# Cross-attention on one core: where in SBUF the scores' weights lie, and a layer norm in place

## What is computed

```
Q = x @ Wq ; K = ctx @ Wk ; V = ctx @ Wv            (per head)
attn = softmax(mask(Q K^T / 16)) ; c = attn V
out = concat_heads(c) @ Wo + x
y = (out - mean(out)) * rsqrt(var(out) + 1e-5) * gamma + beta
```

## Time and profile before

| | |
|---|---|
| median of three executions | 318.01 us |
| the profiled execution's own time | 317.95 us |
| its span in the profile | 316.1 us |
| TensorE busy (weight loads) | 309.5 us (303.4 us) |
| VectorE, ScalarE, GpSimd busy | 253.1, 222.0, 181.3 us |

### The profile page before, as it was taken

The page is one execution under the profiler, slowest core; times in us unless marked ns, Lnnn a source line. Parts: engine busy times, 40 slices in busy tenths (PEclk is TensorE's granted clock), DMA queues, the critical chain, the costliest instruction groups (busy, mean ns, idle before and its releaser), DMA issues.

```text
span 316.1 us, 8051 instructions
## 1 busy us (share of the span) xinstructions
PE 309.5 (98%) x2584; PEld 303.4 (96%) x2584; DVE 253.1 (80%) x721; ACT 222.0 (70%) x601; POOL 181.3 (57%) x183
## 2 busy tenths in 40 slices
PE   8999999999999999999999999999999999999993
PEld 7998889999999999999999999999999999999992
DVE  0467778777999789987998889987998889975686
ACT  2446677768867787678777797678767887777640
POOL 1123476457864587558855586558755686457212
PEclk9999999999999999999999999999999999999998
DMA  7996443564354454384446535364355435440101
GB/s 254 358 400 242 137 150 117 158 218 134 98 163 160 159 175 140 141 239 142 133 126 208 172 133 163 129 214 156 113 187 185 170 100 184 143 155 4 35 0 66
DMA packets 46911, 50.27 MB, mean 159 GB/s; under 512 B 3504, under 2 KB 37040, under 8 KB 46896
## 3 DMA queue, kind: packets, MB, share of 16 engines
q1 hardware_dynamic: 46608, 49.56, 47.0%
q10 hardware_dynamic: 288, 0.52, 0.7%
HBM read 32.24 MB, written 17.83 MB: 158 GB/s over the span
## 4 chain that ended last, share of the span: by engine, by line
PE 95%; DMA 2%; DVE 1%; SPq 1%; POOLq 0%; issue 0%; POOL 0%
PE score_bank L321 25%; PE out_bank L321 19%; PE gL_bank L321 14%; PE tL_bank L321 13%; PE tU_bank L321 9%; PE gU_bank L321 7%; DMA wq_raw<-in_wqT 2%; PE spare_bank L321 1%; PE tL_bank L355 1%; PE spare_bank L355 1%; PE tL_bank L337 1%; PE tU_bank L337 1%; PE out_bank L361 1%; PE tU_bank L361 1%; PE out_bank L337 0%; PE spare_bank L337 0%
## 5 line engine op out<-in xcount | busy, mean ns | idle before, releaser
L1017 POOL TENSOR_TENSOR probs<-probs,inv_sum 128x512 f32<-128x512 f32 x64 | 66.7, 1043 | 84.4 <-DVE inv_sum L804 83.8
L615 ACT ACTIVATE probs<-neg_scores,neg_max 128x256 f32<-128x256 f32 x128 | 64.1, 502 | 36.1 <-DVE neg_max L793 36.0
L1040 POOL TENSOR_TENSOR pT_lo<-pT_raw,pT_hi 128x512 fp32r<-128x512 f32 x60 | 76.6, 1297 | 8.6 <-ACT pT_hi L572 8.6
L793 DVE CUSTOM_DVE_ANT_0 neg_scores<-score_bank,mask_bias 128x256 f32<-128x256 f32 x128 | 49.1, 420 | 6.3 <-PE score_bank L321 3.9
L814 DVE STREAM_TRANSPOSE squares<-probs 128x512 f32<-128x512 f32 x60 | 42.3, 706 | 1.0 <-DMA scratch<-squares 0.8
L572 ACT ACTIVATE tL_hi<-tL_bank 128x512 fp32r<-128x512 f32 x31 | 18.6, 599 | 29.6 <-PE tL_bank L321 29.6
L321 PE MATMUL score_bank<-ctxT_hi,gU 128*128 128x256 f32 x128 | 36.1, 282 | 0.0
L321 PE MATMUL score_bank<-ctxT_hi,gL_lo 128*128 128x256 f32 x128 | 35.9, 281 | 0.0
L321 PE MATMUL score_bank<-ctxT_lo,gU 128*128 128x256 f32 x128 | 35.9, 281 | 0.0
L321 PE MATMUL score_bank<-ctxT_lo,gL_hi 128*128 128x256 f32 x128 | 35.9, 280 | 0.0
L321 PE MATMUL score_bank<-ctxT_hi,gL_hi 128*128 128x256 f32 x128 | 35.6, 278 | 0.0
(11 more groups left out here) (167 smaller groups left out, 981.0 us busy)
## 6 DMA issues: line engine op xcount, KB each, us to landing
scratch<-squares SPq DMA_DIRECT2D x30, 512.0 KB, 2.8
pT_raw<-scratch SPq DMA_DIRECT2D x120, 128.0 KB, 3.1
xT_raw<-in_xT SPq DMA_DIRECT2D x8, 256.0 KB, 4.5
ctxT_raw<-in_ctxT SPq DMA_DIRECT2D x8, 256.0 KB, 4.7
wo_raw<-in_wo SPq DMA_DIRECT2D x4, 512.0 KB, 14.3
x_res<-in_x SPq DMA_DIRECT2D x8, 256.0 KB, 3.2
out<-y_out SPq DMA_DIRECT2D x7, 256.0 KB, 2.6
wq_raw<-in_wqT SPq DMA_DIRECT2D x3, 512.0 KB, 7.6
```

The source lines that it names most:

```text
L615: nc.scalar.activation(probs[j % 2][:, n, :], neg_scores[:, n, :], ACT.Exp, bias=neg_max[:, n:n + 1], scale=-1.0, accum_out=row_sum[:, n:n ...
L793: nc.vector.tensor_tensor_reduce(out=neg_scores[:, n, :], in0=score_bank[hh][:, q, :], in1=mask_bias[:], scale=-SCALE, scalar=3.0e38, op0= ...
L1017: nc.gpsimd.tensor_tensor(probs[j % 2][:, rows, :], probs[j % 2][:, rows, :], inv, ALU.mult) \
L1040: nc.gpsimd.tensor_tensor(pT_lo[j % 2][:, k].rearrange("p hh (q i r) -> p (hh q) i r", q=QT, i=ROWS), pT_raw[j % 2][:, k].rearrange("p i n ...
```

## The change

- The g tiles lose their padding and move ahead of tL_hi, among the other weights, at a remainder of 0. With the 64 bytes of eps_col and power_col left between the weights and all that is streamed, every distance becomes 64 instead of -64.
- Steps 0 to 4 use another buffer for g, `g_early`, which lies right ahead of the streamed tiles at the same remainder as these: distance 0 in their scores.
- The layer norm works in place in `y`: y_scaled and y_out are gone, the store reads `y`, and the wait for the previous store moves from the normalisation to the addition of the residual.
- The last batch's sum, statistics and result are in `y_last`, which now lies in the probabilities' first buffer.

```
-APART = 16
+EARLY = 5
+        gL_hi = sb("gL_hi", [P, 2, S], F32R)
+        gL_lo = sb("gL_lo", [P, 2, S], F32R)
+        gU = sb("gU", [P, 2, S], F32R)
         tL_hi = sb("tL_hi", [P, 2, S], F32R)
...
         power_col = sb("power_col", [P, QT])
-        gL_hi = sb("gL_hi", [P, 2, S + APART], F32R)[:, :, 0:S]
-        gL_lo = sb("gL_lo", [P, 2, S + APART], F32R)[:, :, 0:S]
-        gU = sb("gU", [P, 2, S + APART], F32R)[:, :, 0:S]
+        g_early = sb("g_early", [P, 3, 2, S], F32R)
         xT_hi = sb("xT_hi", [P, IT, S], F32R)
...
         y = sb("y", [P, QT, DI])
-        y_scaled = sb("y_scaled", [P, QT, DI])
-        y_out = sb("y_out", [P, QT, DI])
-        y_last = neg_scores[:, 0:QT, :]
...
+        y_last = probs[0][:, 0:QT, :]
+        def g_tiles(t):
+            if isinstance(t, int) and t < EARLY:
+                return tuple(g_early[:, n] for n in range(3))
+            return gL_hi[:], gL_lo[:], gU[:]
...
-                sp.dma_start(batch_of(out, b), y_out[:]).then_inc(out_stored, 16)
+                sp.dma_start(batch_of(out, b), y[:]).then_inc(out_stored, 16)
...
                 dve.wait_ge(out_product, PAIRS * b + PAIRS)
+                dve.wait_ge(out_stored, 16 * b + 16)
                 nc.vector.tensor_tensor(y[:], out_bank[:], x_res[:], ALU.add).then_inc(out_bank_read, 1)
...
-            def centre_tile(q):
+            def centre_tile(rows, q):
                 nc.vector.scalar_tensor_tensor(
-                    y_scaled[:, q, :], y[:, q, :], mean_var[:, q, 0:1], gamma_sb[:],
+                    rows[:, q, :], rows[:, q, :], mean_var[:, q, 0:1], gamma_sb[:],
...
-            def normalise_tile(b, q, into):
+            def normalise_tile(b, q, rows):
                 nc.vector.scalar_tensor_tensor(
-                    into[:, q, :], y_scaled[:, q, :], rstd[:, q:q + 1], beta_sb[:],
+                    rows[:, q, :], rows[:, q, :], rstd[:, q:q + 1], beta_sb[:],
...
                 dve.wait_ge(rstd_done, b + 1)
-                dve.wait_ge(out_stored, 16 * b + 16)
```

More of the change, by code:

```diff
@@ L384, in scores @@
             def scores(t, j, b, heads=(0, 1)):
+                L_hi, L_lo, U = g_tiles(t)
                 if j == 0:
@@ L395, in scores @@
                         rows = slice(q * P, (q + 1) * P)
-                        hi, lo, up = gL_hi[:, hh, rows], gL_lo[:, hh, rows], gU[:, hh, rows]
+                        hi, lo, up = L_hi[:, hh, rows], L_lo[:, hh, rows], U[:, hh, rows]
                         split_products(score_bank[hh][:, q, :],
@@ L599, in gU_hi_part @@
                 act.wait_ge(g_product, 2 * t + 1)
-                hi_part(gU[0:UP, 0, :], gU_bank[0:UP, 0, :]).then_inc(g_hi_done, 1)
-                hi_part(gU[UP:P, 1, :], gU_bank[UP:P, 0, :]).then_inc(g_hi_done, 1)
+                U = g_tiles(t)[2]
+                hi_part(U[0:UP, 0, :], gU_bank[0:UP, 0, :]).then_inc(g_hi_done, 1)
+                hi_part(U[UP:P, 1, :], gU_bank[UP:P, 0, :]).then_inc(g_hi_done, 1)
             def gL_hi_part(t):
                 act.wait_ge(g_product, 2 * t + 2)
-                hi_part(gL_hi[:], gL_bank[:]).then_inc(g_hi_done, 1)
+                hi_part(g_tiles(t)[0], gL_bank[:]).then_inc(g_hi_done, 1)
             def exponentials(t, j, heads=(0, 1)):
@@ L775, in gU_lo_part @@
                 own, other = (slice(0, UP), slice(UP, P))[::1 if hh == 0 else -1]
-                lo_part(gU[other, hh, :], gU_bank[own, 0, :], gU[own, hh, :]).then_inc(g_split, 1)
+                U = g_tiles(t)[2]
+                lo_part(U[other, hh, :], gU_bank[own, 0, :], U[own, hh, :]).then_inc(g_split, 1)
             def gL_lo_part(t):
                 dve.wait_ge(g_hi_done, 3 * t + 3)
-                lo_part(gL_lo[:], gL_bank[:], gL_hi[:]).then_inc(g_split, 1)
+                L_hi, L_lo, _ = g_tiles(t)
+                lo_part(L_lo, gL_bank[:], L_hi).then_inc(g_split, 1)
             def maxima(t, b, heads=(0, 1)):
@@ L883, in centre @@
                         dve.wait_ge(mean_done, QT * b + QT)
-                    centre_tile(q)
+                    centre_tile(y, q)
             def normalise(b):
                 dve.wait_ge(rstd_done, b + 1)
-                dve.wait_ge(out_stored, 16 * b + 16)
                 for q in range(QT):
-                    normalise_tile(b, q, y_out)
+                    normalise_tile(b, q, y)
             def step(t, j, b, ends=None, folds=()):
@@ L982, in _ @@
                     dve.wait_ge(x_res_in, 16 * B)
-                nc.vector.tensor_tensor(y[:, q, :], output(STEPS - 1, q), x_res[:, q, :], ALU.add) \
+                nc.vector.tensor_tensor(y_last[:, q, :], output(STEPS - 1, q), x_res[:, q, :], ALU.add) \
                     .then_inc(out_bank_read, 1)
                 dve.wait_ge(out_bank_read, B + 1 + q)
-                nc.vector.bn_stats(stats[:, q, :], y[:, q, :]).then_inc(stats_done, 1)
+                nc.vector.bn_stats(stats[:, q, :], y_last[:, q, :]).then_inc(stats_done, 1)
                 dve.wait_ge(stats_done, QT * (B - 1) + 1 + q)
@@ L992, in _ @@
                 dve.wait_ge(mean_done, QT * (B - 1) + 1 + q)
-                centre_tile(q)
+                centre_tile(y_last, q)
             for q in range(QT):
```

## The result

The changed kernel takes 324.75 us (median of four, 324.51 to 324.93) against 318.0; the ratio is 1.021, 95% interval 1.0198 to 1.0222. It is 2.1% slower. The forecast was 315.4; the rival "slow for good" had stood at 324.5.

What follows compares the result with a forecast made beforehand. TensorE, busy 98% of the span, was taken to bound the kernel by its matmul pitch. Terms -2.9 + 0.3 = -2.6 us against the profiled 317.95 gave 315.35, stated as 315.4 for the median; range 314.6 to 321.5.

Steps and rivals of the forecast that it cites:

- slow for good: Rival: scores of steps 0 to 4 hand over the slow rhythm and nothing ends it; 324.5 us, chance 0.15.
- What bounds the kernel, and the two rhythms: TensorE's pitch sets the time; rhythms of 113.3 and 117.6 ns hold themselves; scores' excess costs 0.107 us a step.
- Distance 64 in steps 5 to 31: Scores join the fast rhythm, steps become 8.613 us: -2.9 us, bounds -2.9 and +5.7.
- Distance 0 in steps 0 to 4: 100 early score products at 120.0 ns each: +0.3 us, bounds -0.4 and +0.7.
- What these scores hand over: Step 4's scores at distance 0, followed by query products at 64, were taken to hand over the fast rhythm.
- The sign: Distances outside the scores turn from -64 to 64; fast products at -64 were taken as guide, no separate price.
- VectorE's lead: At step 9's gL_lo load, 0.20 us of lead less 0.17 saved by TensorE leaves 0.03: no wait, cost 0.
- fast throughout: The main case: the fast rhythm holds from the handover on; 314.6 to 316.0 us, chance 0.66.
- The layer norm and the end: Moved store wait never waits, at most some 0.05 us a batch; products behind the final transposes stay slow; 0 taken.
- The rule of two independent read ports: Skill's rule that weight loads take nothing from the running matmul: SBUF places without effect, time stays 318; prediction disagreed.

Runs made afterwards that it cites:

- e1: Changed kernel with g_early padded as before: old mixture of distances in scores of steps 0 to 4, -64 elsewhere; 314.84 to 317.40 us, one execution 323.14.
- e9: e1 plus one needless VectorE addition in step 5 between the low parts of gU and gL, making TensorE wait; 320.09 and 321.43 us.
- e8: e1 with 128 bytes of gap ahead of g_early: same mixture in steps 0 to 4, but distance 64 elsewhere; 324.52 us.
- e10: Changed kernel with 384 bytes of gap ahead of g_early: distance 0 in scores of steps 0 to 4, -64 elsewhere; 324.68 us.
- e5: Changed kernel with distance 0 in scores of steps 0 to 5 (EARLY = 6); five of six executions 323.20 to 323.92 us, one 316.16.
- e14: e1 repeated unchanged; 322.64, 315.02, 315.23, 315.20 and 315.49 us.
- e2: Kernel before with only the in-place layer norm and y_last in the probabilities; 318.08 us, ratio 1.0006.
- e3: Changed kernel with distance 64 in the scores of all steps, 0 to 4 included (EARLY = 0); 324.83 us.
- e7: e1 with the old mixture of distances also in the first step of every batch (g_early where j = 0); 315.86 to 316.23 us, ratio 0.993.
- e4: Changed kernel with distance 0 in the scores of every step (g_early always used); 319.22 us, ratio 1.0037.
- e11: e5 with the layer norm's centring moved behind the low parts of g on VectorE; 325.23 us.
- e6: Changed kernel with distance 0 in step 5's scores alone, distance 64 in all other steps; 323.55 and 323.61 us.
- e12: e1 with the layer norm's centring moved behind the low parts of g on VectorE; 322.66 us.

## Why the prediction was wrong, point by point

- *What bounds the kernel, and the two rhythms.* Right. TensorE's pitch is the time; 113.3 and 117.8 ns both hold themselves, and the 0.107 us a step is there to be had (e1).
- *Distance 64 in steps 5 to 31.* Forecast -2.9 with bounds -2.9 and +5.7; it came out beyond the upper one: +6.01 for the 26 steps between the starts of steps 5 and 31, where the bound gives 26 x 0.21 = +5.5. The slow pitch is 117.8 ns and not the 117.5 that I took from two-digit lengths, which makes 0.231 us a step.
- *Distance 0 in steps 0 to 4.* Forecast +0.3. The five pieces of the chain sum to 12.81 us against 12.58, +0.23. Right.
- *What these scores hand over.* This is the step that failed: "None shows 0 followed directly by 64. I take fast." I had taken distance 0 for a disturbance that ends any rhythm. It has two sequences of its own, and step 4 gets the one that hands over slow: its query products take 1.41 us for 12 and not 1.36, and the steps behind them 8.95 us and not 8.61. The place from which I read that an even run ends fast had a wait between, and e9 shows that such a wait often ends fast by itself. I gave the rival 0.15 though its ground, "nothing ends it any more", stood on rows and my own choice did not. That its 324.5 lies so near the 324.75 is in part luck: it has 0.3 us for slow query products in steps 0 to 3, which were fast, and its steps were priced 0.02 us too low.
- *The sign.* I treated 64 like -64. e8 and e10 show that both the mixture and distance 0 hand over differently to the two.
- *VectorE's lead.* 0.03 us forecast to be left; in e5 and e14 it is used up and TensorE waits 0.02. The sum left out a term: the load starts 0.05 us after gL_lo ends even when TensorE is waiting for it (the kernel before shows it too, in step 1), so 0.20 - 0.17 - 0.05 = -0.02 us. By this the change would have met the wait even with a fast handover, as e5 did, and "fast throughout" at 0.66 was too high on this ground too. In the changed kernel the point never comes up, since its slow steps leave VectorE ahead.
- *The layer norm and the end.* Right (e2; the end is slow as before). The +0.21 us behind the start of step 31 is mostly that step's output and context products, now slow too.
- *The rule of two independent read ports* (the Trainium skill, "TensorE: Matmul & The Clock Gate", section "Step-by-step: what each phase is for"). By it the time would not have moved. The same matmuls at other addresses take 315.2 (most executions of e1 and e14), 318.0 (before) or 324.8 us (after, e3) here.

What stays open is what the phase consists of: no row shows the reads themselves, so why an entry gives one sequence or the other can be tested but not foreseen from these traces. A rival to "distance" also stands untested. The places are worked out from the order of the buffers, and in every kernel here the streamed tiles begin at remainder 64 or 448, both odd multiples of 64. An even distance therefore always goes with weights that begin at an odd multiple of 64 bytes, and the sign with where the streamed tiles lie. No run moves weights and streamed tiles together, so whether the difference counts or the places themselves is not shown.

## What to carry to other kernels

A chain of equal matmuls with a weight load each held either of two pitches for hundreds of products here. Before disturbances are taken away, ask what sets the good rhythm and what sets it again after a wait: here the slower scores of the kernel before were also its repair. A short repair in each round (0.1 us of 34.5) was worth more than the last 0.1 us: e7's six executions have a mean of 316.0 us, the 11 of e1 and e14, without the repair, 316.8. One execution does not show how often a rhythm is lost. And where a lead is worked out from two engines' rows, take off the time from the end of the one's instruction to the start of the other's when it does wait.

## What the runs showed of the hardware that was not expected

- Where the weights being loaded and the streamed operand lie in SBUF changes a matmul's pitch: 113.3 or 117.8 ns at distances of 64 and -64, 120.0 at distance 0 (after, e1, e3, e4). Whether the difference of the two places counts or the places themselves was not tested.
- A wait of 0.02 us on TensorE went with 7.4 us more in one execution (322.64 against 315.2 in most others of the same code); a wait of 0.03 us in another cost nothing more (315.18). A wait can also end the slow rhythm (e11, step 25).
- When TensorE waits for VectorE's gL_lo, its load starts 0.052 to 0.055 us after that instruction ends (e1, e5, e6, e9, e14).
- VectorE's centring takes 2.43 us instead of 1.15 for two instructions beside two GpSimd operations of 2.73 us in all (e12, before).
